# Cross attention and mixture-of-experts layer: low parts of the up weights made during the attention and kept in DRAM, two shared batches behind the experts

## The chip, the cores and the metric

One core of one Trainium2 chip runs the whole program. The metric is the device time of one execution in microseconds (us). The kernel before was timed three times; its profile is of one further execution.

## What is computed

The input x is 4 batches of 512 rows of 256 numbers. Everything is float32.

```python
x = x + attention(layernorm(x), ctx, ctx)      # 16 heads of 16, causal, Sk cut to 512 by the mask
xf = layernorm(x).reshape(2048, 256)
logits = xf @ gate_w.T                          # 8 experts, top 2, softmax over the two
for e in range(8):
    g, u = xf @ wg[e].T, xf @ wu[e].T           # 384 columns each
    out = out + comb[:, e:e+1] * (silu(g) * u @ w_down[e].T)
shared = silu(xf @ sg_gate.T) * (xf @ sg_up.T) @ sg_down.T
x = x + (shared + out)
```

## The kernel before, in words

The program is written by hand for each engine, with semaphores between them; the order of every engine's work is the order of the code. It has four stages.

**Attention.** A prologue, then `batch(b, final)` for b = 0 to 3 (a loop for 0 to 2, the last one apart). A batch is cut into slots, one per group of four heads: g = 1, 2, 3 of this batch and then group 0 of the next. In a slot TensorE (PE) makes the row maxima's scores of the next group ("R" jobs, L624, reduced by VectorE in L1306), the transposed scores of this group ("S" jobs, L644, exponentiated by ScalarE in L1074) and the products with V of the group before ("PV", L654). The slots g = 1 and g = 3 begin with the projection of the next batch's Q and K (L675). VectorE (DVE) takes its result out of PSUM with a bias (`values`, L1254), ScalarE (ACT) makes the first bf16 part of it (`part1`, L1012), and only when `values` has read it may the second R job of the slot write its PSUM pair. The SP queue issues, in the order of the code: the context of the next batch (L412), four groups of 12 transfers that put the bf16 parts into stacks (`stack`, L387), and one third of the down weights per batch (L432).

**Router.** From the second layer norm come logits, the top two experts of each row (a chain of small DVE operations, L1414 to L1467), 0/1 matrices (L1472 to L1483), and a product of these on PE (L898) that gives for each of 39 tiles of 128 slots the row to fetch (`token_of`, L1504). Meanwhile the up weights come from DRAM to `wup` in two transfers of 3 MB (L450); ACT rounds them to fp32r in eight pieces (`hi_parts`, L1150) and DVE subtracts to get the rest (`lo_part`, L1488). Between these PE does the shared expert of batches 0, 1 and 2: `shared_up` (L851, three blocks m of gate and up, float32 matmuls) and `shared_down` (L861). The weights of each row go to DRAM (`who`, L452), and POOL gathers the rows of a tile by an indirect transfer (L580) when these have landed.

**Experts.** For each tile PE multiplies by the expert's up weights in three fp32r products, high by high, high by low, low by high (L923 to L925), and by its down weights likewise (L942 to L944). POOL adds the result to one of two sums in DRAM (L588).

**End.** PE does the shared expert of batch 3. SP loads the two sums (L458, eight transfers of 512 KB), DVE adds them (L1593) and then the shared result of batch 3 (L1606), ACT issues the eight stores of the output (L1211).

Of the kernel before, what the change touches and what calls it, by code (L numbers as in the profile page):

```python
# [28 lines left out]
P = 128  # L29
# [15 lines left out]
def build(nc, x, ctxT, wqT, bq, wkT, bk, wvT, bv, woT, bo, gwT, wupT, wdnT, sgT, suT, sdT, out):  # L45
# [34 lines left out]
    with ExitStack() as ctx:  # L80
# [9 lines left out]
        xn_d = nc.dram_tensor("normed_rows", (N + P, D + WHO), F32, kind="Internal").ap()  # L90
        acc = [nc.dram_tensor(f"sum_rows{i}", (N + P, D), F32, kind="Internal").ap() for i in range(2)]
# [10 lines left out]
        wdn_lo = sb("w_down_lo", [P, M, E * D], F32R)  # L102
        wsg = sb("w_sg", [P, C, HALF])
# [28 lines left out]
        with nc.sbuf_tensor("e_hT_hi", [P, 2, M, P], F32R) as e_hT_hi, \  # L132
                nc.sbuf_tensor("e_hT_lo", [P, 2, M, P], F32R) as e_hT_lo:
            pass
        moe = sb("moe", [P, MOE])
        e_xT_hi = sb("e_xT_hi", [P, 2, C, P], F32R)
# [5 lines left out]
        with nc.sbuf_tensor("ahead_of_router", [P, 24 * KB], F32) as ahead:  # L142
            with nc.sbuf_tensor("router", [P, 24 * KB], F32) as router:
                pass
        ROUTER = 24 * KB
        wup_hi = sb("wup_hi", [P, C, E * 2 * HALF], F32R)
        with nc.sbuf_tensor("wup", [P, C, E * 2 * HALF], F32) as wup:
            pass
        wup_lo = sb("wup_lo", [P, C, E * 2 * HALF], F32R)
        wdn_hi = sb("w_down_hi", [P, M, E * D], F32R)  # L150
# [60 lines left out]
        e_y = xn2T[:, 0, 0:2 * D].rearrange("p (a d) -> p a d", a=2)  # L211
        y_sum = [wup[:, i, 0:T * D].rearrange("p (t d) -> p t d", t=T) for i in range(2)]
        parts_of(router, ROUTER)

        def te():
# [21 lines left out]
        in_tile = part(NJ * NT // 2).bitcast(BF16).rearrange("p (j t) -> p j t", j=NJ)  # L237
# [3 lines left out]
        tcmp = hot[:, NT * E:2 * NT * E].rearrange("p (t e) -> p t e", e=E)  # L241
        at_tile = part(NJ * NCOL * NT // 2).bitcast(BF16).rearrange("p (j c t) -> p j c t", j=NJ, c=NCOL)
# [3 lines left out]
        ld_k, ld_q, ld_ctx, ld_v, ld_o, ld_cv, ld_moe, ld_up = (sem(n) for n in  # L246
            ("ld_k", "ld_q", "ld_ctx", "ld_v", "ld_o", "ld_cv", "ld_moe", "ld_up"))
        consts, pads, fills, pad_rows = sem("consts"), sem("pads"), sem("fills"), sem("pad_rows")
        xn_stored, acc_zeroed = sem("xn_stored"), sem("acc_zeroed")
# [31 lines left out]
        up_hi, up_lo, wts_ready, e_xhi = (sem(n) for n in ("up_hi", "up_lo", "wts_ready", "e_xhi"))  # L281
# [65 lines left out]
        EARLY = 4  # L347

        def piece(w, i):
            cut = C * E * 2 * HALF // SPLITS  # L350
            return w[:].rearrange("p c n -> p (c n)")[:, i * cut:(i + 1) * cut]

# [6 lines left out]
        def _(sp):  # L359
# [77 lines left out]
            with sp.Fori(0, B - 1) as b:  # L437
# [10 lines left out]
            sp.wait_ge(acc_zeroed, 2 * DMA)  # L448
            for c in range(C):
# [12 lines left out]
        def _(pool):  # L462
# [92 lines left out]
            g.iota(tio, [[1, NT], [0, E]], base=0, channel_multiplier=0,  # L555
                   allow_small_or_imprecise_dtypes=True).then_inc(rconsts, 1)
            g.memset(upto, 1.0).then_inc(rconsts, 1)
            pool.wait_ge(rconsts, 5)
# [11 lines left out]
            count(io_np, [[0, 1]], N, 1)  # L570

# [1073 lines left out]
```

## Time and profile before

| | us |
|---|---|
| median of the 3 runs (499.95 to 501.97) | 500.93 |
| the profiled execution | 502.17 |
| its span, first to last instruction | 500.3 |
| PE busy | 458.4 (92%) |
| DVE busy | 308.2 (62%) |
| ACT busy | 210.1 (42%) |
| POOL busy | 193.1 (39%) |
| mean granted clock of TensorE | 0.982 |

Times in the trace run from the start of the span. Attention is 0 to 268, the router stage 268 to 327, the experts 327 to 476, the end 476 to 500. A batch of the attention takes 57.7 us. Times in the rows are starts; a busy time of PE includes the latency of a matmul, so the spacing of two starts tells what one costs.

### The profile page before, as it was taken

To read this page: it belongs to the slowest core of one execution; us is meant where nothing else is said; L and a number is where in the kernel's file an instruction comes from. 1 tells how busy PE (TensorE), PEld (TensorE's weight loads), DVE (VectorE), ACT (ScalarE), POOL (GpSimd) and SP (SyncE) were. 2 spreads that over 40 slices of the span, in tenths; PEclk is the share of its full clock that TensorE was granted. 3 is DMA by queue.
4 is the path that set the end of the run, shared out by engine and by line. 5 is a ranking of instruction groups with operands and counts; after the bars stand their busy time and mean duration, and the time that the engine had idled before them with its cause. 6 is when DMAs were issued, how large, how long until landed. Compare 5 with 4: busy or idle time off the path is not lost.

```text
span 500.3 us, 10299 instructions
## 1 busy us (share of the span) xinstructions
PE 458.4 (92%) x3154; PEld 318.9 (64%) x3155; DVE 308.2 (62%) x651; ACT 210.1 (42%) x420; POOL 193.1 (39%) x204
## 2 busy tenths in 40 slices
PE   7868999999999999988699799999999999999993
PEld 6644344654447443554256366599999999999852
DVE  4984757477563757656674796855554554555436
ACT  2254666517572566517862352523322322322210
POOL 4123545114541336201512002126666766665420
PEclk9998999999999999999979899999999999999998
DMA  8593322422124121400298900014344344444279
GB/s 263 102 229 107 108 72 65 149 65 73 64 78 145 33 95 47 138 28 2 77 371 292 367 2 21 21 33 65 64 74 74 63 71 70 70 65 74 33 197 338
DMA packets 45574, 53.84 MB, mean 108 GB/s; under 512 B 7760, under 2 KB 41872, under 8 KB 44912
## 3 DMA queue, kind: packets, MB, share of 16 engines
q1 hardware_dynamic: 34320, 39.77, 24.8%
q0 software_dynamic: 7488, 10.31, 12.8%
q10 hardware_dynamic: 3744, 3.47, 2.7%
q8 instruction: 13, 0.21, 0.2%
q14 instruction: 9, 0.07, 0.1%
HBM read 27.09 MB, written 13.67 MB: 81 GB/s over the span
## 4 chain that ended last, share of the span: by engine, by line
PE 68%; DVE 10%; ACT 9%; DMA 6%; issue 5%; SPq 1%; DVEq 0%; ACTq 0%; POOLq 0%
PE set_a L624 7%; PE set_b L654 7%; PE set_a L924 6%; PE set_a L925 5%; PE set_a L923 5%; ACT attention L1074 5%; PE set_a L851 5%; PE set_a L675 4%; PE set_b L644 4%; DVE attention L1306 3%; PE set_b L861 3%; PE set_b L942 3%; PE set_a L832 3%; PE set_b L943 3%; PE set_b L944 3%
## 5 line engine op out<-in xcount | busy, mean ns | idle before, releaser
L1306 DVE TENSOR_REDUCE attention<-set_a 128x2 f32<-128x1024 f32 (+2 forms) x96 | 95.9, 1042 | 28.0 <-PE set_a L626 26.1
L1074 ACT ACTIVATE attention<-set_b 128x512 f32<-128x512 f32 (+1 forms) x176 | 88.4, 570 | 58.5 <-PE set_b L644 45.8
L528 POOL TENSOR_SCALAR_AFFINE_SELECT attention<-attention 128x512 f32<-128x512 f32 x64 | 40.8, 650 | 110.4 <-ACT attention L1074 110.4
L588 POOL DMA_INDIRECT sum_rows<-moe,token_of x39 | 61.8, 1585 | 43.9 <-issue 28.9
L644 PE MATMUL set_b<-attention 99*128 99x512 bf16 (+3 forms) x256 | 60.4, 310 | 13.6 <-ACT attention L1074 10.2
L624 PE MATMUL set_a<-attention 96*128 96x512 bf16 (+3 forms) x256 | 61.5, 306 | 5.6 <-DVE attention L1306 5.4
L580 POOL DMA_INDIRECT e_x<-normed_rows,token_of x39 | 39.4, 1010 | 63.7 <-DVE token_of L1504 37.3
L1173 ACT ACTIVATE moe<-set_a 128x384 f32<-128x384 f32 x39 | 19.1, 490 | 104.9 <-PE set_a L925 104.9
L1529 DVE TENSOR_TENSOR moe<-set_a,moe 128x384 f32<-128x384 f32 x39 | 21.8, 558 | 62.7 <-ACT moe L1173 62.7
L624 PEld LDWEIGHTS set_a<-attention 96*128 96x128 bf16 x256 | 25.3, 99 | 45.3 <-DVE attention L1306 18.0
L923 PE MATMUL set_a<-wup_hi,e_xT_hi 128*128 x156 | 53.1, 340 | 0.0
L924 PE MATMUL set_a<-wup_lo,e_xT_hi 128*128 x156 | 52.9, 339 | 0.0
L925 PE MATMUL set_a<-wup_hi,e_xT_lo 128*128 x156 | 52.8, 338 | 0.0
L626 PE MATMUL set_a<-maskb,identb 128*128 128x128 bf16 x256 | 49.6, 222 | 0.0
L654 PE MATMUL set_b<-attention 128*32 128x128 f32 (+3 forms) x512 | 46.2, 463 | 0.4 <-ACT attention L995 0.3
L644 PEld LDWEIGHTS set_b<-attention 99*128 99x128 bf16 x256 | 19.6, 99 | 37.2 <-ACT attention L1074 24.8
L942 PE MATMUL set_b<-w_down_hi,e_hT_hi 128*128 x117 | 36.4, 311 | 1.3 <-DVE moe L1541 0.8
L995 ACT ACTIVATE attention<-set_b 12x512 bf16<-12x512 f32 (+4 forms) x48 | 25.7, 596 | 22.6 <-PE set_b L820 10.2
L509 POOL TENSOR_TENSOR attention<-attention 128x512 f32<-128x512 f32 x14 | 15.9, 1154 | 47.5 <-ACT attention L995 27.8
L944 PE MATMUL set_b<-w_down_hi,e_hT_lo 128*128 x117 | 32.9, 281 | 0.0
L943 PE MATMUL set_b<-w_down_lo,e_hT_hi 128*128 x117 | 32.9, 281 | 0.0
L995 ACT ACTIVATE attention<-attention 128x512 bf16<-128x512 f32 x32 | 19.4, 644 | 30.9 <-DVE attention L1254 26.2
(167 smaller groups left out, 843.5 us busy)
## 6 DMA issues: line engine op xcount, KB each, us to landing
attention<-attention SPq DMA_DIRECT2D x182, 64.0 KB, 2.6
wup<-in_wupT SPq DMA_DIRECT2D x2, 3072.0 KB, 14.6
sum_rows<-attention SPq DMA_DIRECT2D x2, 2048.0 KB, 13.6
wup<-sum_rows SPq DMA_DIRECT2D x8, 512.0 KB, 7.0
attention<-in_ctxT SPq DMA_DIRECT2D x7, 512.0 KB, 6.2
w_down<-in_wdnT SPq DMA_DIRECT2D x3, 1024.0 KB, 5.0
x_res<-in_x SPq DMA_DIRECT2D x4, 512.0 KB, 7.1
out<-x_res ACTq DMA_DIRECT2D x8, 256.0 KB, 4.0
```

The source lines that it names most:

```text
L588: g.indirect_dma_start(acc[i], bass.IndirectOffsetOnAxis(token_of[:, t:t + 1], 0), e_y[:, t % 2, :], None, compute_op=ALU.add).then_inc(ad ...
L624: mm(dst, qstack[0:ROWS, g // 2, h, k * P:w], kstack[0:ROWS, g // 2, h, 0:w], start=True, stop=False)
L626: last = mm(dst[:, k * P:w], identb[:], maskb[:], start=False, stop=True)
L644: last = mm(bank(par)[:, i * w:(i + 1) * w], kstack[0:ROWS + 3, g // 2, h, k * P:(k + 1) * P], qstack[0:ROWS + 3, g // 2, h, k * P:S], sta ...
L654: last = mm(pv_bank[32 * h:32 * h + 32, k * P:S], vaug[:, k, HG * g + h, :], pT[k][:, h, :], start=k == 0, stop=k == QT - 1, tile_position ...
L923: mm(dst, e_xT_hi[:, a, c, :], wup_hi[:, c, cols], start=c == 0, stop=False)
L924: mm(dst, e_xT_hi[:, a, c, :], wup_lo[:, c, cols], start=False, stop=False)
L925: last = mm(dst, e_xT_lo[:, a, c, :], wup_hi[:, c, cols], start=False, stop=c == C - 1)
L942: mm(dst, e_hT_hi[:, a, m, :], wdn_hi[:, m, cols], start=m == 0, stop=False)
L943: mm(dst, e_hT_hi[:, a, m, :], wdn_lo[:, m, cols], start=False, stop=False)
L1074: nc.scalar.activation(pT[k][:, h:h + heads, :], bank(par)[:, 0:heads * (S - k * P)], ACT.Exp).then_inc(b_free, 1)
L1306: v.tensor_reduce(dst, src, AX.X, ALU.max, negate=True).then_inc(a_free, 1)
```

## The change

1. Attention, batches 0 to 2: a third of the up weights (2 MB) is loaded ahead by SP, ACT rounds its four pieces of 128x1024 to fp32r (`ahead_part`), DVE subtracts (`ahead_low`), both in front of `part1` and `values` of the slots g = 1 and behind the maxima of g = 3. The low part takes the place of the loaded third (the tensors share their bytes), is stored to DRAM by SP behind the last stack of the batch, and when that store has landed SP loads the next third. SP's loop over the batches is written out.
2. Router stage: `wup` is loaded in four transfers of 1.5 MB in 2 KB blocks, then `wup_lo` in four more from DRAM. DVE makes no low parts here. The weights of the rows are stored by ACT. The 0/1 matrices lie in another place, so that two writes wait for the last store of normed rows.
3. PE's shared batch 2 goes from the router stage to behind the experts; batch 1's down product is spread around the first transposes.
4. Behind the experts gate and up of batches 2 and 3 are made of fp32r parts, three products for one, whose parts ACT and DVE make in expert slots 4 to 8.

```diff
@@ SP
+            def load_ahead(b):
+                sp.dma_start(ahead[:, 0:C, :], wupT.rearrange("(c p) n -> p c n", p=P)[:, :, b * W_AHEAD:(b + 1) * W_AHEAD]
+                             ).then_inc(ahead_in, DMA)
+
             stack(2, 1)
+            load_ahead(0)
             stack(3, 1)
...
                     sp.wait_ge(b_full, n_b + 3 * B_SLOT)
                     stack(3, 2 * b + 3)
+                    sp.wait_ge(ahead_lo, AHEAD * (b + 1))
+                    sp.dma_start(up_lo_d[:, :, b * W_AHEAD:(b + 1) * W_AHEAD], wdn_hi[:, 0:C, :].bitcast(F32)
+                                 ).then_inc(ahead_out, DMA)
+                    if b + 1 < B - 1:
+                        sp.wait_ge(ahead_out, DMA * (b + 1))
+                        load_ahead(b + 1)
                     sp.dma_start(wdn[:, bass.ds(b, 1), :], wdnT[bass.ds(b * P, P)].rearrange("p (o n) -> p o n", o=1)
                                  ).then_inc(ld_dn, DMA)
...
             for c in range(C):
-                sp.dma_start(wup[:, c, :], wupT[c * P:(c + 1) * P]).then_inc(ld_up, DMA)
-            sp.wait_ge(who_ready, TOP_K)
-            sp.dma_start(xn_d[0:N, D:D + WHO].rearrange("(t p) i -> p t i", p=P), who).then_inc(who_stored, DMA)
+                for turn in range(2):
+                    sp.dma_start(in_blocks(wup[:, c, :], turn), in_blocks(wupT[c * P:(c + 1) * P], turn)
+                                 ).then_inc(ld_up[c], DMA)
+            for c in range(C):
+                for turn in range(2):
+                    sp.dma_start(in_blocks(wup_lo[:, c, :].bitcast(F32), turn), in_blocks(up_lo_d[:, c, :], turn)
+                                 ).then_inc(ld_lo, DMA)
@@ PE
+            def shared_up_parts(b):
                 for m in range(M):
+                    n = b * M + m
+                    pe.wait_ge(s_h, n - 1)
+                    for i, (w_lo, dst) in enumerate(zip((wsg_lo, wsu_lo), gu[n % 2])):
+                        for c in range(C):
+                            high, low = w_hi[:, i, c, m * P:(m + 1) * P], w_lo[:, c, m * P:(m + 1) * P]
+                            rows_hi, rows_lo = x_hi[b - 2][:, c, :], x_lo[:, c, b * S:(b + 1) * S]
+                            mm(dst, high, rows_hi, start=c == 0, stop=False)
+                            mm(dst, high, rows_lo, start=False, stop=False)
+                            last = mm(dst, low, rows_hi, start=False, stop=c == C - 1)
+                    last.then_inc(s_up, 1)
...
             pe.wait_ge(hot_read, 1)
+            shared_down(1, 0, 1)
             rows_t(0, 0, 0, 1, True)
-            shared_up(2, 2, 3)
+            shared_down(1, 1, 2)
             rows_t(1, 1, 1, 1)
-            shared_down(2)
+            shared_down(1, 2)
             pe.wait_ge(experts_known, 1)
             first = [expert(t) for t in range(3)]
-            pe.wait_ge(up_lo, SPLITS)
-            pe.wait_ge(s_h, (B - 1) * M)
+            pe.wait_ge(up_hi, SPLITS)
+            pe.wait_ge(ld_lo, 2 * DMA * C)
+            pe.wait_ge(s_h, (B - 2) * M)
             up(0, 0, first[0])
...
             pe.wait_ge(e_hr, NT)
-            shared_up(3)
+            pe.wait_ge(end_lo, AHEAD)
+            shared_up_parts(2)
             pe.wait_ge(e_yr, NT + 1)
+            shared_down(2)
+            shared_up_parts(3)
             shared_down(3)
@@ ACT
+            def ahead_part(b, k):
+                if k == 0:
+                    act.wait_ge(ahead_in, DMA * (b + 1))
+                if k > 1:
+                    act.wait_ge(ahead_lo, AHEAD * b + k - 1)
+                copy(ahead_high(k), ahead_piece(ahead, k)).then_inc(ahead_hi, 1)
...
                 for g in range(1, NG):
                     u = None
+                    if g != 2 and not final:
+                        ahead_part(b, g - 1)
+                        ahead_part(b, g)
                     if g != 2 and not final:
                         u, job = (2 * b + 2, n_a) if g == 1 else (2 * b + 3, n_a + 2 * A_GRP + 1)
@@ DVE
+            def ahead_low(b, k):
+                dve.wait_ge(ahead_hi, AHEAD * b + k + 1)
+                v.tensor_tensor(ahead_piece(wdn_hi, k), ahead_piece(ahead, k), ahead_high(k),
+                                ALU.subtract).then_inc(ahead_lo, 1)
...
                 n, par = A_PRO + b * A_PER, A_PRO
+                if not final:
+                    ahead_low(b, 0)
+                    ahead_low(b, 1)
...
                     max_parts(n, b * NG + g + 2)
+                    if g == 3 and not final:
+                        ahead_low(b, 2)
+                        ahead_low(b, 3)
...
             for m in range(M):
-                shared_h(3, m)
-                add_sum(1, slice(m * QT, (m + 1) * QT), (y_in[1][m], DMA))
+                shared_h(2, m)
+            for b in range(B - 2):
+                add_sum(1, slice(b * QT, (b + 1) * QT), (y_in[1][b], DMA))
+            shared_y(2)
+            shared_h(3, 0)
+            dve.wait_ge(s_yfree, B)
+            add_sum(1, slice(2 * QT, 3 * QT), (y_in[1][2], DMA))
+            shared_h(3, 1)
             add_sum(1, slice(T - QT, T), (y_in[1][B - 1], DMA))
+            shared_h(3, 2)
             for c in range(2 * B):
```

On the SP queue, from the transfers of a batch's stacks (`attention<-attention`) to the context of the next batch. Before, in the loop:

```order
L387 DMA attention<-attention 16x4x512 x12
L432 ISA
L432 DMA w_down<-in_wdnT 128x2048
L437 REGISTER_ALU
L437 COMPARE_AND_BRANCH
```

Now, of batch 0 and the beginning of batch 1 (`up_low_parts` is the DRAM tensor of the low parts, `up_ahead` the third that is loaded ahead):

```order
L412 DMA attention<-attention 16x4x512 x48
L463 DMA up_low_parts<-w_down_hi 256x1x2048
L430 DMA up_ahead<-in_wupT 128x2x2048
L468 DMA w_down<-in_wdnT 128x2048
L442 DMA attention<-in_ctxT 128x2x512
```

The store and the load stand between the last stack and the down weights, and the context of the next batch is behind them all.

On DVE, the beginning of a batch of the loop, before:

```order
L1379 ISA
L1254 TENSOR_SCALAR attention<-set_a,attention 128x512 x2
L1298 REGISTER_ALU
L1306 TENSOR_REDUCE attention<-set_a 128x2
L1298 REGISTER_ALU
```

And now:

```order
L1413 TENSOR_TENSOR w_down_hi<-up_ahead,w_down_hi 128x1024
L1412 REGISTER_ALU
L1413 TENSOR_TENSOR w_down_hi<-up_ahead,w_down_hi 128x1024
L1337 ISA
L1339 TENSOR_SCALAR attention<-set_a,attention 128x512 x2
L1383 REGISTER_ALU
L1391 TENSOR_REDUCE attention<-set_a 128x2
```

Two subtractions stand in front of the two operations of `values`.

On PE, in front of the first expert, from the 0/1 products (x32) on, before:

```order
L898 MATMUL set_b<-router 128x78 x32
L861 MATMUL set_b<-w_sd,moe 128x256 x12
L851 MATMUL set_a<-moe,w_sg 128x512 x2
L851 MATMUL set_a<-moe,w_su 128x512 x2
L851 MATMUL set_a<-moe,w_sg 128x512 x2
L851 MATMUL set_a<-moe,w_su 128x512 x2
L910 MATMUL set_b<-ident,e_x 128x128 x2
L851 MATMUL set_a<-moe,w_sg 128x512 x2
L851 MATMUL set_a<-moe,w_su 128x512 x2
L910 MATMUL set_b<-ident,e_x 128x128 x2
L861 MATMUL set_b<-w_sd,moe 128x256 x12
```

And now, with one block of gate and up left behind those products:

```order
L959 MATMUL set_b<-moe 128x78 x32
L896 MATMUL set_a<-moe,w_sg 128x512 x2
L896 MATMUL set_a<-moe,w_su 128x512 x2
L921 MATMUL set_b<-w_sd,moe 128x256 x4
L970 MATMUL set_b<-ident,e_x 128x128 x2
L921 MATMUL set_b<-w_sd,moe 128x256 x4
L970 MATMUL set_b<-ident,e_x 128x128 x2
L921 MATMUL set_b<-w_sd,moe 128x256 x4
```

## Rows read from the trace of the kernel before

**Rows 1.** The page: busy time, share of the span and instructions per engine.

```profile
PE 458.4 (92%) x3154; PEld 318.9 (64%) x3155; DVE 308.2 (62%) x651; ACT 210.1 (42%) x420; POOL 193.1 (39%) x204
```

**Rows 2.** Timeline, SP queue: start, duration, issues (prologue's last stacks; end of batch 0).

```profile
32.25 16.45 SPq L387 DMA_DIRECT2D attention<-attention  x24
...
94.46 1.21 SPq L432 DMA_DIRECT2D w_down<-in_wdnT  x1
```

**Rows 3.** DMA issues: engine, count, KB each, median us to landing.

```profile
w_down<-in_wdnT SPq DMA_DIRECT2D x3, 1024.0 KB, 5.0
attention<-in_ctxT SPq DMA_DIRECT2D x1, 512.0 KB, 3.6
```

**Rows 4.** Timeline, DVE, beginnings of slots: start, duration, [idle before <-releaser].

```profile
49.49 1.41 DVE L1254 TENSOR_SCALAR attention<-set_a,attention 128x512 f32<-128x512 f32 x2 [4.97 <-PE set_a L675]
...
105.32 1.41 DVE L1373 BATCH_NORM_STATS2 stats<-x_res  x4
107.19 1.41 DVE L1254 TENSOR_SCALAR attention<-set_a,attention 128x512 f32<-128x512 f32 x2 [0.47 <-PE set_a L675]
...
141.62 1.23 DVE L1306 TENSOR_REDUCE attention<-set_a 128x2 f32<-128x1024 f32 x1 [2.62 <-PE set_a L626]
```

**Rows 5.** Timeline, PE's second R job and ACT's `part1`, batch 1.

```profile
108.66 0.39 PE L624 MATMUL set_a<-attention 96*128 96x512 bf16 x1
...
107.98 1.29 ACT L995 ACTIVATE attention<-attention 128x512 bf16<-128x512 f32 x2 [8.03 <-DVE attention L1254]
```

**Rows 6.** Pieces of 128x1024 of the down weights: duration ns min/median/max.

```profile
L995 ACT ACTIVATE w_down_hi<-w_down x6: 1058/1087/1118, 227.4 to 250.5; 128x1024 fp32r<-128x1024 f32 x6
L1328 DVE TENSOR_TENSOR w_down_lo<-w_down,w_down_hi x6: 1210/1222/1654, 240.0 to 251.6; 128x1024 fp32r<-128x1024 f32 x6
```

**Rows 7.** Stretches: PE, PEld, DVE, ACT, POOL busy, PE's clock, DMA share, GB/s.

```profile
250.00:256.00 6.00, 5.68 (x44) 2.29 (x40) 3.36 (x12) 5.13 (x9) 1.85 (x3) 0.50 1.06 361
...
340.00:360.00 20.00, 19.88 (x138) 19.47 (x137) 11.09 (x32) 5.75 (x15) 13.45 (x11) 1.00 0.44 71
```

**Rows 8.** Timeline, PE, router stage.

```profile
303.75 1.34 PE L898 MATMUL set_b<-router 128*128 128x78 bf16 x32
...
310.18 1.88 PE L851 MATMUL set_a<-moe,w_sg 128*128 128x512 f32 x4
...
321.47 0.41 PE L910 MATMUL set_b<-ident,e_x 128*128 128x128 f32 x2 [0.60 <-DVE e_xT_lo L1515]
...
326.71 0.53 PE L923 MATMUL set_a<-wup_hi,e_xT_hi 128*128 x1
```

**Rows 9.** Timeline, DVE and POOL, router stage.

```profile
299.06 1.39 DVE L1483 TENSOR_SCALAR router<-router 128x128 bf16<-128x128 bf16 x8
...
307.12 0.24 DVE L1504 TENSOR_SCALAR token_of<-router 128x39 int32<-128x39 f32 x1
...
308.30 1.15 POOL L580 DMA_INDIRECT e_x<-normed_rows,token_of  x1 [37.27 <-DVE token_of L1504]
```

**Rows 10.** Landing of the two loads of `wup` (L450, from 268.4), and stretches with their GB/s.

```profile
DMA to landing us min/median/max: 10.3/14.6/18.8
...
276.00:280.00 4.00, 3.62 (x8) 1.44 (x8) 3.56 (x13) 0.92 (x1) 0.00 (x0) 1.00 1.00 429
...
483.00:487.00 4.00, 4.00 (x13) 2.01 (x12) 3.05 (x3) 1.09 (x2) 0.00 (x0) 1.00 1.11 345
```

**Rows 11.** Timeline, PE, fp32r products of 384 columns (nine starts lie between).

```profile
327.08 0.34 PE L924 MATMUL set_a<-wup_lo,e_xT_hi 128*128 x1
...
328.84 0.34 PE L925 MATMUL set_a<-wup_hi,e_xT_lo 128*128 x1
```

**Rows 12.** Timeline, PE and DVE, the end.

```profile
476.01 1.88 PE L851 MATMUL set_a<-moe,w_sg 128*128 128x512 f32 x4
...
486.31 5.34 PE L861 MATMUL set_b<-w_sd,moe 128*128 128x256 f32 x24
...
495.84 1.28 DVE L1606 TENSOR_TENSOR x_res<-set_b,x_res 128x512 f32<-128x512 f32 x2
```

More of the change, by code:

```diff
@@ L134, in build @@
             pass
+        with nc.sbuf_tensor("moe_parts", [P, MOE], F32R) as moe_r:
+            pass
         moe = sb("moe", [P, MOE])
+        ROUTER = 2068
+        with nc.sbuf_tensor("router", [P, ROUTER], F32) as router:
+            pass
         e_xT_hi = sb("e_xT_hi", [P, 2, C, P], F32R)
@@ L139, in build @@
         e_w = sb("e_w", [P, 2, TOP_K])
[L142 to L146, printed above, removed]
         with nc.sbuf_tensor("wup", [P, C, E * 2 * HALF], F32) as wup:
             pass
+        wup_hi = sb("wup_hi", [P, C, E * 2 * HALF], F32R)
         wup_lo = sb("wup_lo", [P, C, E * 2 * HALF], F32R)
+        with nc.sbuf_tensor("up_ahead", [P, M, E * D], F32) as ahead:
+            pass
         wdn_hi = sb("w_down_hi", [P, M, E * D], F32R)
@@ L436, in _ @@
             sp.dma_start(xn_d[N:N + P, :], zeros).then_inc(pad_rows, DMA)
-            with sp.Fori(0, B - 1) as b:
+            for b in range(B - 1):
                 batch(b, False)
@@ L892, in _ @@
             shared_down(0)
-            shared_up(1)
+            shared_up(1, 0, 2)
             pe.wait_ge(hot_built, 1)
@@ L900, in _ @@
             last.then_inc(hot_full, 1)
-            shared_down(1)
-            shared_up(2, 0, 2)
+            shared_up(1, 2)
             def rows_t(t, a, x, filled, first=False):
@@ L1145, in shared_silu @@
                 act.wait_ge(s_up, b * M + m + 1)
-                nc.scalar.activation(sg[:, m, :], gate[(b * M + m) % 2], ACT.Silu).then_inc(s_sg, 1)
+                h = sg if b < B - 2 else sg_end
+                nc.scalar.activation(h[:, m, :], gate[(b * M + m) % 2], ACT.Silu).then_inc(s_sg, 1)
             def hi_parts(pieces):
@@ L1192, in slot @@
                 silu(t, a)
-            with act.Fori(0, (NT - 5) // 2) as i:
+            PEEL = 9
+            high_of = ((x_hi[0], xn2T[:, :, 2 * S:3 * S]), (x_hi[1], xn2T[:, :, 3 * S:4 * S]),
+                       (w_hi[:, 0], wsg[:]), (w_hi[:, 1], wsu[:]))
+            for t in range(3, PEEL):
+                slot(t, t % 2)
+                if t - 4 in range(AHEAD):
+                    copy(*high_of[t - 4]).then_inc(end_hi, 1)
+            with act.Fori(0, (NT - 2 - PEEL) // 2) as i:
                 for j in range(2):
-                    slot(2 * i + 3 + j, (3 + j) % 2)
+                    slot(2 * i + PEEL + j, (PEEL + j) % 2)
             slot(NT - 2, (NT - 2) % 2)
@@ L1201, in _ @@
             hidden_t(NT - 1, (NT - 1) % 2)
-            for m in range(M):
-                shared_silu(3, m)
+            for b in range(B - 2, B):
+                for m in range(M):
+                    shared_silu(b, m)
             o_t = out.rearrange("b (k p) d -> p (b k) d", p=P)
@@ L1571, in slot, with end_low @@
                 hidden(t, a)
[L1573 to L1575 removed]
+            def end_low(i):
+                dve.wait_ge(end_hi, i + 1)
+                dst, src, high = ((x_lo[:, :, 2 * S:3 * S], xn2T[:, :, 2 * S:3 * S], x_hi[0]),
+                                  (x_lo[:, :, 3 * S:4 * S], xn2T[:, :, 3 * S:4 * S], x_hi[1]),
+                                  (wsg_lo[:], wsg[:], w_hi[:, 0]), (wsu_lo[:], wsu[:], w_hi[:, 1]))[i]
+                v.tensor_tensor(dst, src, high, ALU.subtract).then_inc(end_lo, 1)
+            PEEL = 9
+            for t in range(3, PEEL):
+                slot(t, t % 2, (t + 1) % NX, freed(t - 3) if t > 4 else None)
+                if t - 5 in range(AHEAD):
+                    end_low(t - 5)
+            LOOPS = (NT - 1 - PEEL) // NX
             with dve.Fori(0, LOOPS) as i:
                 for j in range(NX):
[L1578 to L1579 removed]
+                    slot(NX * i + PEEL + j, (PEEL + j) % 2, (PEEL + 1 + j) % NX,
+                         (added[j % 2], DMA * (2 * i + 2 + j // 2 + 1)))
+            for t in range(PEEL + NX * LOOPS, NT - 1):
                 slot(t, t % 2, (t + 1) % NX, freed(t - 3))
```

116 lines of the change are left out of this document (63 added, 53 removed).

## The prediction

> **What bounds the kernel now.** I read the page first: PE is busy 92% of the span, the next engine 62% [rows 1]. So the first question of every part is what it does to PE's queue, and only then who else is late. In the expert stage PE is busy 19.88 us of 20 at full clock while DVE is busy 11.09 and ACT 5.75 [rows 7]: there only PE's own work counts. The timelines then show where PE is not the only limit: the beginnings of the attention's slots, where its second R job starts at 108.66, right behind DVE's `values`, 107.19 plus 1.41 [rows 4, 5]; the router stage, where from 303.75 on it runs its own queue with one idle spot of 0.60 [rows 8]; and the end, where the shared result is added at 495.84, some 4 us after PE's last product at 486.31 plus 5.34 [rows 12]. The last number is slack: at the end the loads of the sums are the limit, not PE.
>
> **The attention: the third that comes too late.** SP now issues, where the down weights are issued at 94.46 [rows 2], first the store of a third's low parts (2 MB), then waits until it has landed, and only then issues the load of the next third (2 MB) into the same bytes. A load of 512 KB lands after 3.6 us, one of 1024 KB after 5.0 [rows 3]: 1.4 us per 512 KB and 2.2 fixed, so 7.8 us for 2 MB, twice. Everything before it in SP's queue is the same as before. The third of batch 1 is there at 94.5 + 7.8 + 0.2 + 7.8 = 110.3. But ACT stands in front of `part1` from about 100 on (8.03 us idle ahead of 107.98) and DVE in front of `values` from 106.7, when its statistics end [rows 4, 5]. Now ACT must copy a piece (1.09 us) and DVE subtract two (1.22 each) [rows 6] before `values`: 110.3 + 1.1 + 2.4 = 113.8 where it started at 107.19. That is 6.6 us later, and PE's second R job, which waits for it, is 6.6 us later too. Queued behind ACT's copies are `part1` and the exponentials, behind DVE's the row maxima; they all shift by the same and PE, the busiest engine, has nothing with which to make it up. Batch 2 repeats this: 13.2 us. With 429 GB/s [rows 10] for the data and the same fixed part the two transfers take 7.1 each, the loss is 5.2 per batch; with 345 [rows 10] it is 7.6.
>
> Batch 0's third is issued in the middle of 24 stack transfers that go out from 32.25 for 16.45 us [rows 2]: 40.5 + 7.8 = 48.3, and 48.3 + 1.1 + 2.4 = 51.8 against 49.49 [rows 4], 2.3 us. If it lands 2.3 sooner it costs nothing, if the stacks ahead of it hold it up 4.
>
> Pieces 2 and 3 of a batch cost nothing: on DVE they fall into the 2.62 us of idle ahead of 141.62 [rows 4] with 2 times 1.22; on ACT 2.2 us go ahead of the `part1` of g = 3, which waits for PE's projection; at worst half a us per batch.
>
> PE then stands idle for over 6 us in one piece. There is a stretch, 250 to 256, in which the granted clock is 0.50, 1.2 GHz, although PE is busy 5.68 us of 6 [rows 7]; it follows the attention's last slots, where PE waited often. If the clock falls so after each of the two waits, PE does 3 us of work in 6 and loses up to 3 us each; DVE paces the R jobs in part of it. I take 1.5 each, 3.0 together, between 0 and 6.
>
> The other transfers: the context of the next batch is now behind 2 MB and 1 MB and lands some 10 us later, but is needed half a batch later. The loop of SP that is written out costs SP nothing that anybody waits for.
>
> **The router stage.** PE loses `shared_up(2)` and `shared_down(2)`: from 310.18 to the first expert product at 326.71 are 16.5 us, of which two pairs of transposes, 0.2 each, stay [rows 8]. So PE could begin at 310.6, 16.1 sooner, the idle 0.60 included. Who could be late instead? The list of rows: the 0/1 matrices are ready at 299.06 + 1.39 [rows 9], the products take 1.3, `token_of` follows at 302.1 in place of 307.12, the first gather 1.2 later at 303.3 [rows 9], and PE comes to its first transposes at 301.8 + 3.4 + 1.7 = 307.0: just in time. The loads: before, 6.3 MB of up weights and 0.5 MB of normed rows had landed 18.8 us after 268.8 [rows 10], 6.8 MB / (18.8 - 2.2) = 410 GB/s. Now 13.1 MB: 268.8 + 32.0 + 2.2 = 303.0, and the many small writes of `who` beside them add up to 4: 307 against the 310.6 at which they are needed. At 345 GB/s [rows 10], the worst rate of a read in small blocks here, they land at 309 to 313. DVE's low parts of the up weights (eight of 1.75) vanish, but DVE was not what PE waited for. I take 0.7 for these near meetings: -15.4, between -16.1 and -12.
>
> The Trainium skill (DMA: Bandwidth & Descriptors, Specifications) limits one core's DRAM traffic to about 358 GB/s, which would speak against reading the low parts back: 13.1 MB would take 36.6 us. The trace does not agree in this very stretch: 429 GB/s from 276 to 280 [rows 10]. By the page the loads would land at 307.6 to 311.6 and the sum would be up to 1.0 us dearer.
>
> **The expert stage.** ACT and DVE make four pairs of parts in slots 4 to 7 and 5 to 8, 1.1 and 1.2 us each, beside 5.75 and 11.09 busy us of 20 [rows 7]. What they delay is needed a slot later. 0.3 us, between 0 and 1.2.
>
> **The end.** PE now does two shared batches. An fp32r product of 384 columns takes (328.84 - 327.08) / 10 = 0.176 us [rows 11], one of 512 then 0.235; gate and up of a batch are 36 of them, 8.5 us, where the float32 ones took 486.31 - 476.01 = 10.3 [rows 12]. The down product is as before, 5.2. Two batches: 27.3 from 476.0 on, so PE ends at 503.3 where it ended at 491.5: 11.8 later. The slack of 4 us is used up in part: behind the last block of gate and up (498.1) DVE has the product with silu (ready at 499.6) and then, as its queue is ordered, all eight sums of 0.65 us (two take the 1.28 of the row at 495.84 [rows 12]), and only then the shared result: 504.8 against 495.84. +9.0, between 7.7 (only PE counts) and 10.
>
> **The sum.** 2.3 + 13.2 + 3.0 - 15.4 + 0.3 + 9.0 = +12.4 us. Against the profiled execution of 502.17 that is 514.6. It ran 1.2 above the median, so the median comes to 500.93 + 12.4 = 513.3. With the bounds of the unknown terms it lies between 504 and 522.
>
> **Rivals.** *The thirds come in time.* If store and load together take under 11 us in place of 15.8, the third of batch 1 is there by 105.6, ACT's copies lie in its 8.03 us of idle, and only DVE's two pieces stand between its statistics (106.7) and `values`: 1.9 us per batch, 5.7 in all, or nothing if PE makes that up from the few per cent in which it idles in the attention. No clock loss. The sum is then 5.7 - 15.4 + 0.3 + 9.0 = -0.4, 500.5, down to -6.1, 494.8. For it: the load need not wait for more than the data, and the DMA queues are nearly idle there. Against: the two landings of [rows 3] are of undisturbed transfers, and 11 us for both would be 5.5 for 2 MB, hardly more than 1 MB takes.
>
> *The up weights' low parts come late.* At 345 GB/s and with the small writes of `who` they land at 313, the gathers that share the queues take their part, and `who` itself may land after 303.3 and hold back the first gather. PE then waits 3 to 5 us more ahead of the first expert: 517.
>
> **How the numbers follow.** The forecast has 0.62, the first rival 0.23 (0.14 of it faster, 0.09 about the same), the second 0.15. A measurement here tells 0.5%, 2.5 us, from no change: 498.4 to 503.4. With a little of the forecast's lower edge the chances are 0.14, 0.10 and 0.76. The range from 499 to 521 leaves out the faster part of the first rival and the far end of both others.
>
> **What would show it.** Right: ACT's first copy of batches 1 and 2 released by the DMA of `up_ahead`, 15 to 16 us after the issue of the store; PE's longest idle spots in front of the second R job of these batches, about 6 us; a granted clock under 1 behind them; the first expert product 15 us sooner after the router's beginning; 27 us of PE behind the last tile, and DVE's shared result about 29 us behind it. Wrong: `values` released by PE as before, or a wait of PE for `ld_lo` of several us, or an end that is less than 7 us longer.

## The result and the profile after

The changed kernel takes 520.07 us in the median of four runs (518.09 to 521.73). The kernel before, run beside it, takes 500.44 (499.86 to 501.97). The ratio is 1.0386, with a 95% interval from 1.0341 to 1.043: slower by 3.9%, 19.6 us. The profiled execution took 519.79, and its span 517.8. That is 17.5 more than the span of before; the other 2 us come from which execution was profiled (before's ran 1.7 above its median here, after's 0.3 below). The runs of one kernel lie some 3 us apart.

The page of the changed kernel: busy time and count of each engine, TensorE's granted clock in 40 slices, the chain of waits, and DMA issues with KB each and us to landing.

```profile
PE 460.2 (89%) x3178; PEld 325.0 (63%) x3179; DVE 314.0 (61%) x659; ACT 225.3 (44%) x436; POOL 197.7 (38%) x204
...
PEclk9998899996999979999997999999999999999999
...
PE 57%; DVE 12%; DMA 11%; ACT 9%; issue 6%; SPq 4%; ACTq 0%; DVEq 0%; POOLq 0%
...
up_ahead<-in_wupT SPq DMA_DIRECT2D x3, 2048.0 KB, 8.1
up_low_parts<-w_down_hi SPq DMA_DIRECT2D x3, 2048.0 KB, 7.8
...
wup_lo<-up_low_parts SPq DMA_DIRECT2D x4, 1536.0 KB, 18.8
```

Against [rows 1] PE is busy 1.8 us more and the span is 17.5 longer, so most of the loss is not PE's work but its standing idle: 11% of the chain is now DMA, 6% before. The 2 MB transfers land after 7.8 and 8.1 us, as the working had it (7.8).

The stages, from PE's starts in the two traces:

| from the span's start to | before | after | gained or lost in the stage |
|---|---|---|---|
| router stage (its second block of gate and up) | 276.38 | 298.74 | attention +22.4 |
| first expert product | 326.71 | 334.42 | router stage −14.7 |
| first product of the end | 476.01 | 485.54 | experts +1.8 |
| DVE adds the last shared result | 495.84 | 513.76 | end +8.4 |
| end of the span | 500.3 | 517.8 | stores −0.4 |

The first block of gate and up starts at 268.46 before and at 290.95 after: 22.5 later, so the place of the border changes nothing.

**The attention.** Timeline of the changed kernel, SP queue (start, duration; the issue, not the landing), batch 0 and the beginning of batch 1:

```profile
40.74 0.59 SPq L430 DMA_DIRECT2D up_ahead<-in_wupT  x1
41.38 8.21 SPq L412 DMA_DIRECT2D attention<-attention  x12
...
98.96 0.90 SPq L463 DMA_DIRECT2D up_low_parts<-w_down_hi  x1
107.92 0.38 SPq L430 DMA_DIRECT2D up_ahead<-in_wupT  x1
```

The timeline of ACT, DVE and PE there, with the idle time ahead of each and what ended it:

```profile
49.44 2.00 ACT L1060 ACTIVATE w_down_hi<-up_ahead 128x1024 fp32r<-128x1024 f32 x2 [1.96 <-DMA up_ahead<-in_wupT]
54.63 1.15 ACT L1060 ACTIVATE attention<-attention 128x512 bf16<-128x512 f32 x2 [3.19 <-DMA attention<-attention]
54.26 0.39 PE L669 MATMUL set_a<-attention 96*128 96x512 bf16 x1 [3.37 <-DVE attention L1339]
...
116.05 2.00 ACT L1060 ACTIVATE w_down_hi<-up_ahead 128x1024 fp32r<-128x1024 f32 x2 [11.54 <-DMA up_ahead<-in_wupT]
117.14 2.36 DVE L1413 TENSOR_TENSOR w_down_hi<-up_ahead,w_down_hi 128x1024 fp32r<-128x1024 f32 x2 [5.81 <-ACT w_down_hi L1060]
119.41 1.41 DVE L1339 TENSOR_SCALAR attention<-set_a,attention 128x512 f32<-128x512 f32 x2
120.87 0.61 PE L669 MATMUL set_a<-attention 96*128 96x512 bf16 x1 [7.62 <-DVE attention L1339]
...
186.34 0.61 PE L669 MATMUL set_a<-attention 96*128 96x512 bf16 x1 [5.15 <-DVE attention L1339]
```

Read the batch 1 rows from the top, with the SP rows above: the store goes out at 98.96 and has landed 8.95 us later, the load goes out at 107.92 and lands 8.10 later, and in that moment ACT copies (116.05), then DVE subtracts (117.14), then come `values` (119.41) and PE (120.87). Nothing in this chain has any slack. Batch 2 repeats it from 166.88 with landings of 7.05 and 7.54. PE stands idle for 3.37, 7.62 and 5.15 us where [rows 5] had its R job right behind `values`: 16.1 us together. In batches 1 and 2 the R job of 512 columns behind the wait takes 0.61 where [rows 5] has 0.39, and the windows show why.

Windows of the changed kernel, columns as in [rows 7]:

```profile
112.00:116.00 4.00, 1.26 (x10) 0.16 (x8) 0.00 (x0) 0.00 (x0) 0.00 (x0) 1.00 1.01 422
116.00:120.00 4.00, 0.00 (x0) 0.00 (x0) 2.86 (x3) 2.00 (x2) 0.00 (x0) 0.61 0.62 250
120.00:124.00 4.00, 3.13 (x15) 0.94 (x16) 3.17 (x4) 1.26 (x2) 2.27 (x2) 0.50 0.15 51
124.00:128.00 4.00, 4.00 (x25) 2.47 (x24) 2.48 (x3) 1.54 (x3) 0.00 (x0) 0.61 0.14 48
128.00:132.00 4.00, 3.23 (x37) 1.48 (x35) 2.06 (x6) 4.00 (x10) 2.20 (x3) 1.00 0.00 0
...
188.00:192.00 4.00, 4.00 (x21) 1.72 (x14) 2.50 (x3) 0.86 (x2) 0.73 (x1) 0.50 0.25 82
```

In all these windows the trace of before has a clock of 1.00. Here it falls to 0.50, 1.2 GHz, while PE stands idle, and stays there for some 6 us after PE has begun again. From the projection in slot g = 1 to the one in g = 3 batch 1 takes 33.7 us (108.11 to 141.83) in place of 23.5, 10.2 more, of which 7.6 are idle: the low clock costs 2.6. Reckoned in the same way (176.04 to 207.01, and 45.65 to 73.91 in place of 23.6) it costs 2.3 in batch 2 and 1.3 in batch 0. The halves of a batch behind these have the same length in both traces. So of the attention's 22.4 us 16.1 are idle and 6.2 the low clock, all in these three places.

**The router stage.** The changed kernel's timeline of PE, POOL and DVE there, and the landing of the loads of the low parts:

```profile
322.85 1.36 PE L959 MATMUL set_b<-moe 128*128 128x78 bf16 x32 [0.81 <-DVE moe L1581]
...
325.69 1.15 POOL L625 DMA_INDIRECT e_x<-normed_rows,token_of  x1 [32.18 <-DVE token_of L1595]
...
330.41 0.44 PE L970 MATMUL set_b<-ident,e_x 128*128 128x128 f32 x2 [0.96 <-DMA e_x<-normed_rows,token_of]
...
334.42 0.43 PE L983 MATMUL set_a<-wup_hi,e_xT_hi 128*128 x1
```

```profile
L495 SPq DMA_DIRECT2D wup_lo<-up_low_parts x4: 2696/4558/6968, 298.2 to 313.2; - x4
...
DMA to landing us min/median/max: 16.8/18.8/20.9
```

PE waits for the 0/1 matrices and for the gather, 1.8 us together; another 0.64, ahead of a down product at 313.18, is for DVE's product with silu. The last load of low parts, issued at 313.2, has landed by 330.0, 4.4 us before the first expert product, and nothing waits for it.

**The end.** Timeline of PE's last down product, and of DVE, in the changed kernel:

```profile
507.51 5.34 PE L921 MATMUL set_b<-w_sd,wup 128*128 128x256 f32 x24
...
508.34 0.69 DVE L1502 TENSOR_TENSOR wup<-set_a,wup 128x512 f32<-128x512 f32 x1 [0.98 <-ACT wup L1223]
508.95 4.89 DVE L1685 TENSOR_TENSOR x_res<-x_res,wup 128x512 f32<-128x512 f32 x8
513.76 1.28 DVE L1705 TENSOR_TENSOR x_res<-set_b,x_res 128x512 f32<-128x512 f32 x2
```

PE has ended by 512.9. The eight sums in DVE's queue go on until 513.8: DVE is the later of the two, by about 1 us.

### The profile page after: what moved, and what is told of

It reads as the page before. It is cut to its first block, busy times and chain, and to the rows that moved or that the text cites. A ratio compares the mean times of both kernels' runs of the same rounds, so it can differ in the third digit from the quotient of the medians.

```text
span 517.8 us, 10306 instructions
## 1 busy us (share of the span) xinstructions
PE 460.2 (89%) x3178; PEld 325.0 (63%) x3179; DVE 314.0 (61%) x659; ACT 225.3 (44%) x436; POOL 197.7 (38%) x204
## 3 DMA queue, kind: packets, MB, share of 16 engines
q1 hardware_dynamic: 39872, 58.62, 33.7%
## 4 chain that ended last, share of the span: by engine, by line
PE 57%; DVE 12%; DMA 11%; ACT 9%; issue 6%; SPq 4%; ACTq 0%; DVEq 0%; POOLq 0%
PE set_a L669 6%; PE set_a L983 5%; PE set_a L984 5%; PE set_a L985 5%; PE set_b L699 5%; DMA up_ahead<-in_wupT 5%; ACT attention L1147 4%; PE set_b L689 3%; SPq L412 3%; PE set_b L1002 3%; DMA up_low_parts<-w_down_hi 3%; PE set_b L1004 3%; PE set_b L1003 3%; PE set_b L993 2%; DVE attention L1391 2%
## 5 line engine op out<-in xcount | busy, mean ns | idle before, releaser
L572 POOL TENSOR_SCALAR_AFFINE_SELECT attention<-attention 128x512 f32<-128x512 f32 x64 | 43.2, 687 | 110.9 <-ACT attention L1147 110.9
L669 PE MATMUL set_a<-attention 96*128 96x512 bf16 (+3 forms) x256 | 65.8, 322 | 21.7 <-DVE attention L1339 16.1
L689 PE MATMUL set_b<-attention 99*128 99x512 bf16 (+3 forms) x256 | 62.1, 316 | 13.6 <-ACT attention L1147 9.5
L669 PEld LDWEIGHTS set_a<-attention 96*128 96x128 bf16 x256 | 26.4, 103 | 62.2 <-DVE attention L1339 21.4
L671 PE MATMUL set_a<-maskb,identb 128*128 128x128 bf16 x256 | 51.8, 230 | 0.0
L689 PEld LDWEIGHTS set_b<-attention 99*128 99x128 bf16 x256 | 19.9, 100 | 38.0 <-ACT attention L1147 24.9
L1060 ACT ACTIVATE attention<-set_b 12x512 bf16<-12x512 f32 (+4 forms) x48 | 25.7, 596 | 21.6 <-PE set_b L865 10.2
L671 PEld LDWEIGHTS set_a<-maskb,identb 128*128 128x128 bf16 x256 | 26.6, 104 | 6.2 <-issue 4.4
## 6 DMA issues: line engine op xcount, KB each, us to landing
wup<-in_wupT SPq DMA_DIRECT2D x4, 1536.0 KB, 14.6
sum_rows<-attention SPq DMA_DIRECT2D x2, 2048.0 KB, 13.3
```

The source lines that it names most:

```text
L669: mm(dst, qstack[0:ROWS, g // 2, h, k * P:w], kstack[0:ROWS, g // 2, h, 0:w], start=True, stop=False)
L671: last = mm(dst[:, k * P:w], identb[:], maskb[:], start=False, stop=True)
L689: last = mm(bank(par)[:, i * w:(i + 1) * w], kstack[0:ROWS + 3, g // 2, h, k * P:(k + 1) * P], qstack[0:ROWS + 3, g // 2, h, k * P:S], sta ...
```

## The experiments

The theory: PE loses its time in the attention because the copies and subtractions of a third stand in front of `part1` and `values` and the third lands too late; the slow clock follows the idle. The rivals: the work of the pieces itself is too much for ACT and DVE; the traffic of the added transfers costs it, wherever the pieces stand. The first two experiments move one thing each.

### Pieces 0 and 1 one slot later

```diff
@@ ACT
-                    if g != 2 and not final:
-                        ahead_part(b, g - 1)
-                        ahead_part(b, g)
+                    if g != 1 and not final:
+                        ahead_part(b, 2 * g - 4)
+                        ahead_part(b, 2 * g - 3)
@@ DVE
-                if not final:
-                    ahead_low(b, 0)
-                    ahead_low(b, 1)
...
-                    if g == 3 and not final:
-                        ahead_low(b, 2)
-                        ahead_low(b, 3)
+                    if g in (2, 3) and not final:
+                        ahead_low(b, 2 * g - 4)
+                        ahead_low(b, 2 * g - 3)
```

> The changed kernel with the first two pieces of each third moved one slot on: ACT copies them at the beginning of slot g = 2 instead of g = 1, DVE subtracts them behind the maxima of g = 2. Same work, same transfers, same end; only the wait for the third is gone from the batch's beginning. Theory (the third comes too late, PE stands idle and its clock falls): the three waits of 3.4, 7.6 and 5.2 us and the slow stretches behind them, 1.2, 2.6 and 2.1, go, 520.1 - 22.1 = 498.0, up to 501 if the copies hold up the exponentials of g = 2. Rival A (it is the inserted work of ACT and DVE that costs, wherever it stands): 515 or more. Rival B (only the wait, the clock has nothing to do with it): 504.

Measured: 500.17 us (498.43 to 501.74, ten runs), ratio to before 0.9965, 0.9948 to 0.9982. All the loss is gone, with the same transfers and the same pieces (ACT's copies now stand at the beginning of g = 2, DVE's subtractions behind the maxima of g = 2). The first rival falls, as does the wait without the clock (504, above all ten runs), and the second falls as the cause of the loss; a part of it is left in batch 0, as the rows show. The timelines of ACT and PE in this kernel, and its windows:

```profile
55.38 1.15 ACT L1060 ACTIVATE attention<-attention 128x512 bf16<-128x512 f32 x2 [9.49 <-DMA attention<-attention]
...
57.07 0.61 PE L689 MATMUL set_b<-attention 99*128 99x512 bf16 x1 [3.70 <-ACT attention L1147]
```

```profile
56.00:60.00 4.00, 2.93 (x17) 1.58 (x21) 1.30 (x5) 3.59 (x9) 2.90 (x3) 0.57 0.24 79
60.00:64.00 4.00, 4.00 (x36) 1.94 (x38) 0.10 (x1) 3.09 (x7) 2.87 (x3) 0.58 0.22 72
120.00:124.00 4.00, 3.43 (x30) 1.08 (x28) 1.82 (x2) 3.12 (x7) 3.00 (x4) 1.00 0.26 85
```

In batch 1 the clock is 1.00 again without anything done to it. From the first projection to the router stage are 236.2 us (43.97 to 280.13), in the changed kernel 253.1 (45.65 to 298.74): 16.9 less, while the idle spots shrank from 16.1 to 3.7, by 12.4. The other 4.5 are the low clock: the 2.6 and 2.3 of batches 1 and 2 are gone, and batch 0 loses 1.8 behind its 3.70 of idle where it lost 1.3. What is left in batch 0 is a second mechanism, which the changed kernel has too: the twelve stack transfers stand behind the 2 MB load in SP's queue (the load goes out at 41.44 here), and ACT waits for their rows. Those issued from 41 to 46 land after up to 7.9 us, where the kernel before has 2.4 to 2.8.

### The store ahead of the last stack

```diff
@@ SP
                     sp.wait_ge(b_full, n_b + 3 * B_SLOT)
-                    stack(3, 2 * b + 3)
                     sp.wait_ge(ahead_lo, AHEAD * (b + 1))
                     sp.dma_start(up_lo_d[:, :, b * W_AHEAD:(b + 1) * W_AHEAD], wdn_hi[:, 0:C, :].bitcast(F32)
                                  ).then_inc(ahead_out, DMA)
+                    stack(3, 2 * b + 3)
```

> The changed kernel with SP's store of the low parts issued ahead of the batch's last group of stack transfers instead of behind it; the pieces stay at the beginning of g = 1. The store then lands while SP issues the 12 transfers (some 10 us), and the next third is there about 8 us sooner, before DVE ends its statistics. Theory: batches 1 and 2 lose only what DVE's two pieces take, 1.9 us each, batch 0 loses 4.5 as now: 520.1 - 10.2 - 7.3 + 3.8 = 506.4. Rival A (the inserted work costs, not the lateness): 518 to 520. Rival C (2 MB ahead of the stack transfers makes these late and PE waits for the rows): 510 to 520, with a wait of PE for rows in the next batch's slot g = 2.

Measured: 509.99 us (509.4 to 511.15, four runs), ratio 1.017, 1.0147 to 1.0193: 10.1 us faster than the changed kernel, 3.6 slower than expected. The SP queue and ACT:

```profile
91.49 0.57 SPq L462 DMA_DIRECT2D up_low_parts<-w_down_hi  x1
92.10 11.62 SPq L412 DMA_DIRECT2D attention<-attention  x12
103.77 0.58 SPq L430 DMA_DIRECT2D up_ahead<-in_wupT  x1
...
111.66 2.00 ACT L1060 ACTIVATE w_down_hi<-up_ahead 128x1024 fp32r<-128x1024 f32 x2 [7.03 <-DMA up_ahead<-in_wupT]
```

The store went out 7.5 us sooner, but the load only 4.2: SP needed 11.62 us to issue the twelve stack transfers behind the store, 0.97 each, where [rows 2] have 0.69, although the store had landed after 7.1. PE's idle spots are 3.27, 3.10 and 1.87. The last is what two pieces on DVE take, as expected of a third that is in time; batch 1's third is still late. PE has no wait of 1 us or more between these spots, so the rows themselves are not late. So the loss does follow the landing, and SP's issue became the next limit.

### The end in float32

The float32 version of gate and up at the end, with no parts made in the slots, in the changed kernel:

```diff
@@ PE
-            shared_up_parts(2)
+            shared_up(2)
...
-            shared_up_parts(3)
+            shared_up(3)
@@ ACT
-                if t - 4 in range(AHEAD):
-                    copy(*high_of[t - 4]).then_inc(end_hi, 1)
@@ DVE
-                if t - 5 in range(AHEAD):
-                    end_low(t - 5)
```

> The changed kernel with gate and up of batches 2 and 3 behind the experts in float32 as before, without the parts that ACT and DVE make for it in the expert slots. Theory: each of the six blocks takes 3.44 us in place of 2.8, +3.7 us at the end, and the expert slots get back the 1.4 us that the parts cost: 522.4. Rival (the fp32r products are no cheaper, or DVE's sums hide them): 518.7.

Measured: 520.51 us (518.23 to 522.58, four runs), ratio 1.0358, 1.0316 to 1.040. By its time it can't be told from the changed kernel: the idle of batch 0, which the edit does not touch, is 5.55 us in this profile and 3.37 in the other. The timing is inconclusive; the stages of the trace are not. The end takes 32.0 us (484.52 to 516.54) in place of 28.2, and the experts 149.5 in place of 151.1. The edit was made again, below, on a kernel without the stalls.

### Up weights in whole rows of 24 KB

```diff
@@ SP
             for c in range(C):
-                for turn in range(2):
-                    sp.dma_start(in_blocks(wup[:, c, :], turn), in_blocks(wupT[c * P:(c + 1) * P], turn)
-                                 ).then_inc(ld_up[c], DMA)
+                sp.dma_start(wup[:, c, :], wupT[c * P:(c + 1) * P]).then_inc(ld_up[c], DMA)
             for c in range(C):
-                for turn in range(2):
-                    sp.dma_start(in_blocks(wup_lo[:, c, :].bitcast(F32), turn), in_blocks(up_lo_d[:, c, :], turn)
-                                 ).then_inc(ld_lo, DMA)
+                sp.dma_start(wup_lo[:, c, :].bitcast(F32), up_lo_d[:, c, :]).then_inc(ld_lo, DMA)
```

> The changed kernel with the up weights and their low parts loaded in whole rows of 24 KB (two transfers each) instead of 2 KB blocks (four each). Theory (a queue's turn on a DMA engine is a whole descriptor, so short rows of the ACT queue wait for long ones): the last normed rows land 17 to 30 us after their issue instead of 9.5, the rows' weights later than 16.3 us, DVE's 0/1 matrices or the first gather wait for them, and the first expert comes 5 to 15 us later: 525 to 535. Rival (the block size does nothing but cost rate): 518 to 520, the loads at 410 GB/s in place of 385.

Measured: 533.37 us (533.02 to 534.71, four runs), ratio 1.0635, 1.0611 to 1.0659, 13.3 us slower than with the 2 KB blocks. DMA issues of this kernel; DVE and PE:

```profile
wup<-in_wupT SPq DMA_DIRECT2D x2, 3072.0 KB, 13.8
wup_lo<-up_low_parts SPq DMA_DIRECT2D x2, 3072.0 KB, 29.5
...
normed_rows<-moe ACTq DMA_DIRECT2D x1, 512.0 KB, 30.8
```

```profile
326.72 1.46 DVE L1570 TENSOR_TENSOR moe<-moe,router 128x1248 bf16<-128x1248 bf16 x1 [12.81 <-DMA normed_rows<-moe]
...
336.54 2.26 PE L955 MATMUL set_b<-moe 128*128 128x78 bf16 x32 [13.70 <-DVE moe L1577]
```

The loads themselves are faster (windows of 4 us from 296 to 316 show 412 to 443 GB/s, those of the changed kernel 326 to 402). But 512 KB of normed rows, issued on ACT's queue, land after 30.8 us in place of 9.5 (16.6 in the kernel before, which had whole rows too, but no low parts to load), DVE waits 12.81 for them, because the 0/1 matrices take their place, and PE waits 13.70. So the blocks are no detail: they buy the other queue its share. The Trainium skill (DMA: Bandwidth & Descriptors, Queues, rings and completion order) says that each DMA engine takes turns between queues, but drains a whole packet of one before it switches. These two runs agree with it in direction: the same bytes were moved in pieces of 24 KB (and in half as many transfers), and the queue with 1 KB rows waited three times as long. How long a turn is they do not show.

### The first load behind the stacks

On top of the later pieces:

```diff
@@ SP
             stack(2, 1)
-            load_ahead(0)
             stack(3, 1)
+            load_ahead(0)
```

> e1 (pieces moved one slot on) with the load of the first third issued behind the prologue's last stack transfers instead of between them. In e1 PE waited 3.7 us in batch 0 for exponentials that stood behind `part1`, and this for the stack rows that were queued behind the 2 MB. Theory: that wait goes too, 500.2 - 3.7 = 496.5, about 1% under the kernel before. Rival (the rows were late for another reason, or the third, needed from 64 on, now comes too late): 500.

Measured: 497.96 us (496.15 to 500.08, ten runs), ratio 0.9933, 0.9912 to 0.9954. PE's idle spot of batch 0 is gone from this profile, and the kernel is 3.3 us faster than before (501.28 in these runs). This beats both kernels. The kernel with only the pieces moved and this one differ by 2.2 in their medians, less than the 3.7 of the idle spot alone, and their runs overlap.

The wait is not gone from every execution. This profile has a clock of 0.50 from 38 to 48, so that PE comes late to batch 0. Two kernels of the next section have the same attention and a clock of 1.00 there, and both still wait in batch 0; PE in the first of them:

```profile
64.35 0.39 PE L689 MATMUL set_b<-attention 99*128 99x512 bf16 x1 [2.16 <-DMA attention<-attention]
```

The second waits 2.54 us at 64.95, and both have a clock of 0.50 to 0.53 behind it; from the projection in g = 1 to the one in g = 3 they take 26.7 and 27.2 us in place of 23.6. The next stack transfers, now the ones behind the 2 MB load, land after 6.7 to 7.7 us where they are issued from 52 to 56, in place of 2.8 to 3.0. So the edit made the wait shorter and moved it, and in the profile of this kernel PE came too late to meet it.

### The sums sooner, batch 2 in the router stage, and the end in float32 again

Three edits on that version. The first puts DVE's sums ahead of the last blocks' products:

```diff
@@ DVE
             add_sum(1, slice(2 * QT, 3 * QT), (y_in[1][2], DMA))
-            shared_h(3, 1)
             add_sum(1, slice(T - QT, T), (y_in[1][B - 1], DMA))
-            shared_h(3, 2)
+            shared_h(3, 1)
             for c in range(2 * B):
+                if c == 3:
+                    shared_h(3, 2)
```

> e5 with DVE's sums at the end in another order: the last sum of the first kind goes ahead of the product of block (3, 1), and three of the eight sums of the second kind go ahead of the product of (3, 2). Theory (the end is PE's 27.3 us plus a second in which DVE still adds): 0.9 us less than e5, and no more, since PE's last product then is the limit: 495.6. Rival (the stores of the output are the limit): same as e5.

Measured: 497.82 us (496.2 to 498.82, six runs), ratio 0.993, 0.9906 to 0.9954: not to be told from the version it is made on. In the trace of this kernel DVE's last addition is now released by PE:

```profile
491.92 1.29 DVE L1703 TENSOR_TENSOR x_res<-set_b,x_res 128x512 f32<-128x512 f32 x2 [0.85 <-PE set_b L921]
```

It follows PE's last product (486.54) by 5.4 us, where it followed by 6.25 without the edit (486.24 to 492.49). The 0.9 us are there, as the reading of the end had it, but below what the timing resolves.

The second puts shared batch 2 back into the router stage, in float32, and leaves only batch 3 at the end:

```diff
@@ PE
+            shared_down(1)
+            shared_up(2, 0, 2)
             pe.wait_ge(hot_read, 1)
-            shared_down(1, 0, 1)
             rows_t(0, 0, 0, 1, True)
-            shared_down(1, 1, 2)
+            shared_up(2, 2, 3)
             rows_t(1, 1, 1, 1)
-            shared_down(1, 2)
+            shared_down(2)
...
             pe.wait_ge(end_lo, AHEAD)
-            shared_up_parts(2)
-            pe.wait_ge(e_yr, NT + 1)
-            shared_down(2)
             shared_up_parts(3)
```

> e5 with the shared expert of batch 2 back in the router stage, in float32 (PE, ACT and DVE in the order of the kernel before); only batch 3 is behind the experts, from fp32r parts. The parts of batch 2's rows are still made and not used. Theory (PE is the limit of the router stage, so what is moved out of it is saved, and the end is paid by PE's 13.7 us per batch less the slack of 4): the first expert comes 14 to 15 us later than in e5, the end is 8 to 9 shorter, e5 + 6.4 = 503. Rival (the router stage was shortened by the low parts that DVE no longer makes, and the move only lengthens the end): e5 - 5, 491 to 494.

Measured: 503.78 us (501.86 to 505.84, ten runs), ratio 1.005, 1.0034 to 1.0066, 5.8 slower than the version it is made on. From the router stage's beginning to the first expert product are 49.7 us (279.61 to 329.33) in place of 35.2, from the end's beginning to the shared result 19.7 (479.73 to 499.42) in place of 28.2. Moving batch 2 is thus a true gain of the change, of about 6 us, as the terms −15.4 and +9.0 say. The low parts kept in DRAM bring nothing by themselves: with them, and batch 2 where it was, the router stage takes 49.7 us where the kernel before took 50.3, and the whole kernel 2.5 us more, 1.1 of them in the expert slots. Whether batch 2 could be moved without them is untested. In the kernel before DVE made the last low part until 325.6; experts that begin 35.2 us after the stage's beginning would there begin at 311.6.

The third is the float32 end of above:

> e5 with gate and up of batches 2 and 3 at the end in float32 and without their parts in the expert slots (e3 again, on a kernel without the attention's waits, which vary from run to run). Theory: +3.7 at the end, -1.4 in the expert slots: e5 + 2.3 = 498.8. Rival (the fp32r parts bring nothing): e5 or less.

Measured: 500.65 us (498.17 to 501.96, ten runs), ratio 0.9992, 0.9971 to 1.0014, 2.7 slower than with the parts. The end takes 32.0 us again (460.86 to 492.89) and the experts 149.2 (from 311.71) against 151.0 in the version it is made on. So the fp32r parts give 3.8 us at the end and cost about 1.8 in the slots; net 2.0 by the traces, 2.7 by the times.

## Why the prediction was right, and where its sizes were off

The sign, the mechanism and the range held (513.3, from 499.0 to 521.0, against 520.07), the range by 0.9 us: one of the four runs, 521.73, lies above it. The sum came out 6.8 us too low in the median; 5.1 of that are in the span of the traces, the rest lies between the profiled executions and the medians. Term by term:

| term | predicted | trace |
|---|---|---|
| batch 0's third | +2.3 | +3.4 |
| thirds of batches 1 and 2 | +13.2 | +12.8 (7.6 and 5.2) |
| slow clock | +3.0 | +6.2 |
| router stage | −15.4 | −14.7 |
| expert slots | +0.3 | +1.8 |
| end | +9.0 | +8.4 |
| sum | +12.4 | +17.9 (span +17.5, with −0.4 at the stores) |

- **The late thirds** were read rightly, each link of the chain. 15.8 us from the store's issue to the data was the estimate, 17.1 and 14.6 the measured values. The rival that they come in time needed under 11.
- **The clock** is the term that was mis-sized most, by 3.2 us. I took half of a bound that I had worked out as "up to 3 us each" for two waits. The cost was 2.6 and 2.3, nearer to the bound than to half, and both were gone in the experiment that took these waits away. A third wait, batch 0's, which I had not counted as one, cost 1.3. The trace of before had a stretch at 0.50 [rows 7], but no row that spoke for half.
- **Batch 0** was costed by its own third alone, and the sentence that the stacks "ahead of it" might hold it up looked to the wrong side: the stacks behind the load are what is held up. With the pieces moved away PE still waited 3.70 us there. In the changed kernel both waits fall on the same time, which hides the second one. The time differs between executions: 3.4 and 5.6 in two profiles of the same attention. In the first the clock was 0.55 to 0.60 from 38 to 42 and PE came later to this place; in the second it was 1.00.
- **The router stage** was right within 0.7, in part by luck. PE idled more than the 0.7 that I took for near meetings: 0.81 for the 0/1 matrices, 0.96 for the gather and 0.64 for DVE. The loads cost nothing. Against that, one shared block took 3.5 us (305.39 to 308.93) in place of 5.2 (283.03 to 288.27 before), since the clock there was at its higher level, and the prediction had no such term: without these 1.7 us the stage would have gained 13.0. All loads had landed 39.1 us after the first issue, against 38.2 predicted. The limit of 358 GB/s (the Trainium skill, DMA: Bandwidth & Descriptors, Specifications) did not hold in this stretch either: the seven windows of 4 us from 300 to 328 show 372 to 402 GB/s. By it the loads would have ended 38.8 to 42.8 us after the issue, and 39.1 lies in that too, so the end of the loads alone does not tell the two apart. The rival of late low parts is refuted: they had 4.4 us to spare.
- **The expert slots** were mis-sized by 1.5. That ACT has only 5.75 busy us of 20 [rows 7] says nothing of when it is needed: the five slots from the first copy on took 4.54, 3.93, 3.81, 4.01 and 4.36 us in place of 4.10, 3.72, 3.74, 3.72 and 3.84, 1.5 more together. Both kernels without the parts have 149.2 to 149.5 us of experts.
- **The end** was right within 0.6, with the eight sums in DVE's queue as the last limit, as said; moving them made PE the limit.

The price of a wrong place is plain: with the pieces where they stood the kernel takes 19.9 us more than with them one slot later.

## What to carry to other kernels

When work that depends on a transfer is put into the queue of a busy chain, work out the landing from the queue of the engine that issues it, every transfer and every wait ahead of it included, and put it behind the point where it must be there; also look at what is queued behind the big transfer. Add to each idle spot of several us on PE the slower clock behind it: here 16 us of idle in three spots cost another 6. And a mean busy share of 30% does not make a copy in a chained slot free: count it, unless a wait in that slot has room for it.

## What the hardware showed that was not expected

- Two queues that share the DMA engines do not share them evenly when their pieces differ: 512 KB in 1 KB rows landed after 9.5 us beside loads in 2 KB blocks, after 30.8 beside loads in rows of 24 KB.
- Small transfers behind a large one on the same queue land late: 64 KB took 6.7 to 7.7 us behind a 2 MB load, 2.6 elsewhere. Their issue can slow down too: twelve took 11.62 and 10.68 us to issue behind a 2 MB store to DRAM, but 8.21 behind a 2 MB load.
- The same 2 MB store landed after 8.95 us in one batch and 7.05 in the next.
- The low clock often follows PE's idle and stays longer than it: behind 7.62 us of idle the windows read 0.50 and 0.61 for 8 us, with PE at work, and behind 3.70 us of idle (the kernel with the pieces moved) 0.57 and 0.58 for 8 us. In the changed kernel 2.6, 2.3 and 1.3 us were lost behind 7.6, 5.2 and 3.4, but with the store sooner 1.3 behind 1.87 too: there a wait of under 2 us was enough.
- The same idle spot is not always followed by it: behind 1.56 us ahead of a shared block the clock read 0.53 and 0.61 for 4 us in the kernel before, and 1.00 in the changed one.
